# A decoder with mixture-of-experts routing: GpSimd's row transfers issued in gated fours

## The reference, cut to what matters

```python
x = x + L0_ffn(layernorm(x))        # 16 experts, top 4 of a token, and one shared expert
# inside: top_vals, top_idx = top_k(softmax(h @ router_w.T), 4)
#   comb[n, e] = weight of expert e for token n
#   y[e] = silu(h @ w_gate[e]) * (h @ w_up[e]) @ w_down[e]
#   routed = sum over e of y[e] * comb[:, e];  out = routed + sigmoid(h @ sh_gate_w) * shared
x = x + L1_attn(layernorm(x))       # 16 heads of 16 channels
x = x + L1_xattn(layernorm(x), ctx) # keys and values from ctx
x = x + L1_ffn(layernorm(x))
```

## Time and profile before

| | us |
|---|---|
| timed runs, median of 3 | 1796.05 |
| timed runs, lowest to highest | 1793.11 to 1799.43 |
| profiled execution, its own time | 1811.18 |
| profiled execution, span of its instructions | 1809.4 |
| PE busy in it | 1610.7 (89%) |
| DVE busy | 1128.6 (62%) |
| ACT busy | 972.1 (54%) |
| GpSimd busy | 540.4 (30%), with 128 row transfers |

### The profile page before, as it was taken

The page is one execution under the profiler, slowest core; times in us unless marked ns, Lnnn a source line. Parts: engine busy times, 40 slices in busy tenths (PEclk is TensorE's granted clock), DMA queues, the critical chain, the costliest instruction groups (busy, mean ns, idle before and its releaser), DMA issues. The chain is left out here.

```text
span 1809.4 us, 25838 instructions
## 1 busy us (share of the span) xinstructions
PE 1610.7 (89%) x8598; PEld 1292.1 (71%) x8598; DVE 1128.6 (62%) x2496; ACT 972.1 (54%) x2789; POOL 540.4 (30%) x447
## 2 busy tenths in 40 slices
PE   6999989989988868799998869999789999999866
PEld 4888877878877656677776637777668888788634
DVE  4655685776687585354443564544357788777878
ACT  4645545545445544223323546678746666667756
POOL 2233332553363462221103356354021122211000
PEclk9999999999999989999999958898789999999989
DMA  8153344433543052153434311000031110000001
GB/s 274 36 176 128 112 142 137 141 129 105 192 154 120 30 163 76 47 149 113 124 105 129 99 47 38 21 1 24 1 137 30 32 41 33 13 1 1 1 1 47
DMA packets 87511, 151.50 MB, mean 84 GB/s; under 512 B 9940, under 2 KB 45396, under 8 KB 87380
## 3 DMA queue, kind: packets, MB, share of 16 engines
q1 hardware_dynamic: 81236, 133.07, 22.6%
q0 software_dynamic: 6144, 16.79, 2.9%
HBM read 90.84 MB, written 58.98 MB: 83 GB/s over the span
## 5 line engine op out<-in xcount | busy, mean ns | idle before, releaser
L2598 ACT ACTIVATE cross_attention_heads<-cross_attention_heads,small 128x128 f32<-128x128 f32 x256 | 99.6, 390 | 89.3 <-DVE small L2033 89.3
L2342 ACT ACTIVATE self_attention<-self_attention,small 128x128 f32<-128x128 f32 x256 | 99.9, 392 | 79.7 <-DVE small L1666 79.7
L1126 PE MATMUL bank<-cross_attention,cross_attention_heads 128*128 128x256 f32 x512 | 125.0, 387 | 15.3 <-DVE residual L2047 10.1
L790 PE MATMUL bank<-self_attention 128*128 128x256 f32 x512 | 122.2, 381 | 17.4 <-ACT self_attention L2355 9.1
L2702 POOL CAST qkv_weights_split<-self_attention 128x1024 fp32r<-128x1024 f32 x45 | 49.2, 1093 | 253.4 <-DMA self_attention<-in_wqkv 231.4
L595 PE MATMUL bank<-x_channel_major,qkv_weights_split 128*128 128x512 f32 x256 | 117.1, 458 | 7.6 <-DVE qkv_weights_split L1698 2.9
L1126 PEld LDWEIGHTS bank<-cross_attention,cross_attention_heads 128*128 128x128 f32 x512 | 95.9, 192 | 38.8 <-DVE residual L2047 19.0
L2510 ACT ACTIVATE narrow_late<-bank,small 128x128 f32<-128x128 f32 x256 | 91.1, 376 | 58.8 <-DVE small L1904 58.3
L790 PEld LDWEIGHTS bank<-self_attention 128*128 128x128 f32 x512 | 95.5, 190 | 35.7 <-DVE residual L1680 13.8
L2704 POOL TENSOR_TENSOR qkv_weights_split<-self_attention,qkv_weights_split 128x1024 fp32r<-128x1024 f32 x45 | 109.1, 2423 | 3.7
L888 PE MATMUL bank<-experts,tiles 128*128 x316 | 108.0, 465 | 0.4 <-DVE tiles L1782 0.4
(11 more groups left out here) (398 smaller groups left out, 4716.2 us busy)
## 6 DMA issues: line engine op xcount, KB each, us to landing
picked_inputs<-self_attention SPq DMA_DIRECT2D x64, 512.0 KB, 6.7
self_attention<-in_wqkv SPq DMA_DIRECT2D x48, 512.0 KB, 6.1
experts_far<-picked_inputs SPq DMA_DIRECT2D x79, 128.0 KB, 2.1
picked_outputs<-tiles SPq DMA_DIRECT2D x79, 128.0 KB, 1.7
self_attention<-in_wo SPq DMA_DIRECT2D x16, 512.0 KB
experts<-in_moe SPq DMA_DIRECT2D x4, 1408.0 KB
self_attention<-in_bv SPq DMA_DIRECT2D x16, 256.0 KB, 5.7
context_values<-context_out SPq DMA_DIRECT2D x16, 256.0 KB
```

The costliest lines, as they stand in the source:

```text
L790: m = T.matmul(bank[7][:, 0:D], ZT_a[n % 2][:, h, :], wo_a[p % 2][:, h, :], start=h == 0, stop=h == HG - 1)
L1126: m = T.matmul(bank[7][:, 0:D], ZT_x[n % 2][:, h, :], x_wo[hg % 2][:, h, :], start=h == 0, stop=h == HG - 1)
L2342: m = S.activation(P_a[u][:, h, :], P_a[u][:, h, :], ACT.Exp, bias=negmax_a[u][:, h:h + 1], accum_out=sums_a[u][:, h:h + 1])
L2598: m = S.activation(P_x[u][:, h, :], P_x[u][:, h, :], ACT.Exp, bias=negmax_x[u][:, h:h + 1], accum_out=sums_x[u][:, h:h + 1])
```

## The change

Two waits are added to GpSimd's program. `scatter(g, b)` first waits until all transfers of the batches before b, from the start of the dispatch, have landed. In the loop over `gather(0)` to `gather(6)`, each but the first is preceded by a wait until the batch before has landed whole. `slow_scatter`, gather 7 and 8 and the later single picks stay as they are.

```diff
             def scatter(g, b):
+                pool.wait_ge(scattered, 16 * TOPK * (g * GB + b))
                 for k in range(TOPK):
                     scatter_pick(g, b, k)
...
             for bb in range(7):
+                if bb:
+                    pool.wait_ge(gathered[(bb - 1) % NYG], 16 * TOPK * ((bb - 1) // NYG + 1))
                 gather(bb)
```

## The result

| | before | after |
|---|---|---|
| median of 20 timed runs each | 1793.49 us | 1800.62 us |
| lowest to highest | 1790.04 to 1801.75 | 1789.28 to 1807.09 |
| ratio after/before, 95% interval | | 1.003 (1.0016 to 1.0044) |
| profiled execution, own time (span) | 1811.18 (1809.4) | 1795.7 (1793.9) |

The timed runs became 0.3% longer (5.4 us by the ratio), while the profiled execution became 15.5 us shorter. Both are true.

The account below looks back on a forecast made before the run. TensorE, busy 89% of a 1809.4 us span, was taken to bound the kernel. The forecast was 1796.05 - 0 for the gaps + 0 to 1 for the waits, rounded to 1796.0 us, range 1784 to 1802.

Parts of the forecast that it names:

- the price of the waits: Fourteen waits before scatters and gathers on GpSimd: 1.86 us each with work in flight, 0 to about 2 us altogether.
- group 2, +0.57 taken as 0: Expert-loop scatters: only the last batch follows closely, +0.57 us; taken as 0, or 0.6 if nothing hides it.
- the gathers, 0 to 1: Waits ahead of gathers 1 to 6, before the second self-attention: mostly covered, cost 0 to 1 us.
- one landing of 2.83 us: Issue to landing of a row transfer, read at gather 8's fourth transfer and used for every gated batch.
- the account of the gaps: Late waits after long rows of scatters and gathers: most timed executions lack them, they come with the profile's recording.
- the agreement it stood on: Profiled execution less its two gaps, 1811.18 - 15.4 = 1795.8 us, was close to the timed median of 1796.05.
- The size of the gaps, 15.4 us: Excess waits after sixteen scatters (4.1 us, TensorE) and twenty gathers (11.35 us, VectorE), together 15.4 us.
- Rival 1: The gaps are in timed runs too and fours cure them: 1781 to 1790 us; chance 0.28.
- Group 3, 0,: Three effective waits in group 3's scatters, 1.86 us each, covered by TensorE's remaining expert units: cost 0.
- rival 2: Landing is slower than thought, gathers reach past square(0): +5.1 us at 4.0 us landing, 1801 to 1804; chance 0.14.
- Rivals 3 and 4: 3: gap lasts as long as GpSimd issues, 1805 us or more, chance 0.05. 4: waits do nothing, 1796, chance 0.03.

Follow-up runs that it names:

- after_third: The changed kernel, unchanged, run again on a chip where the kernel before shows no gaps: 1799.35 us against 1793.98, ratio 1.0017.
- before_fourth: The kernel before, unchanged, run again on a chip where it shows no gaps: 1793.16 us against 1793.98, ratio 0.9989.

## Why the prediction was wrong

The time of 1800.62 us lies in the stated range, but no change was forecast, with 0 to 1 us for the waits, and the change cost 5.4 us (2.9 to 7.9 by the interval).

**The step that failed is the price of the waits**, in two terms: group 2, +0.57 taken as 0, is 2.2 (point 4), and the gathers, 0 to 1, are 2.6 (point 6). Both stood on one landing of 2.83 us, where it is 5.3 and 3.3. A second step, the account of the gaps, failed beside it (point 1), but what was drawn from it, that the timed runs have none, holds for this first measurement; that was luck in the chip.

1. **"Most timed executions don't have them, they come with the recording"** failed as an account, together with the agreement it stood on: 1811.18 less 15.4 is 1795.8, near the median of 1796.05. On chips A and B the timed runs are as long as the profiled ones, 1808.56 us and more. The profile of before has the gaps (own time 1811.18, below the middle of chips A and B but within their span), and the timed runs are like those of C and D. That they came from two kinds of chip is an inference, for those chips aren't known, and a change with time would fit as well. The agreement itself was luck in its size, since the gaps are worth 21.2 us, and a chip without them gave a profiled span of 1788.4.

2. **The size of the gaps, 15.4 us**, was a term too small by 5.8. For the first I took 6.97 less the 2.90 of the turn before it; the same turn costs 1.25 without a gap, and another 2.2 us is lost behind it, at the lower clock. For the second I counted to the eleventh key bias (11.35 where the whole row loses 13.1).

3. **Rival 1**, that fours cure gaps which timed runs have, is what happens on chip A: 0.9923, less than all of the gaps for the price of the waits. The case against it was point 1. In the first measurement it isn't what decided, as there was nothing to cure.

4. **Group 2, +0.57 taken as 0**, was mis-sized: 2.2. I used the landing of a gather in a quieter stretch, 2.83, where these scatters land in 5.3. The prediction itself put the price at 0.6 if nothing hides it, and took 0 without a row that showed something hiding it; of the 3.2 us for which GpSimd stands, 2.2 reach TensorE. The stretches of after_third say what stands beside them, the last two numbers being DMA share and GB/s:

```profile
640.00:660.00 20.00, 15.11 (x66) 11.10 (x65) 15.13 (x15) 8.66 (x13) 15.40 (x14) 1.00 1.13 295
...
720.00:760.00 40.00, 38.75 (x173) 30.85 (x172) 19.11 (x54) 12.13 (x21) 16.70 (x17) 1.00 0.20 66
```

The DMA engines are full in the first (share 1.13, 295 GB/s) and lightly used in the second (0.20), where group 3 lands in 2.36. The split behind group 2's last four on GpSimd then starts late, as the prediction named.

5. **Group 3, 0,** was right. Its three waits are 1.70 each (1.86 said), and its cover holds: from the L852 near 710 us to the first L879 it is 55.2 us both in after and in before_fourth.

6. **The gathers, 0 to 1,** are 2.6, and the mechanism is rival 2's. I put its point of decision at a pitch of 7.27 us, a landing of 3.16; measured were 7.42 and 3.3, beside a DMA share of 0.44 to 0.55 in the stretches of after. As it said, square(0) comes right behind the last gather and combine(3) waits (3.01 us). By its own sum the squares come 1.0 us late at this pitch (972.58 + 6 x 7.42 + 4.76 = 1021.9, less 1018.5 and 2.4) and gather 3 lands 3.1 us past 998.8; the 2.6 lie between. So a rival with a chance of 0.14 decided this term, on 0.5 us of landing that I could have bracketed: the row used lies in a stretch with less DMA work (share 0.29 from 1052 to 1060). What spoke against it, that gather 9 stood behind the row used, was no match for the loads beside the first seven.

7. **Rivals 3 and 4** are out: the gap doesn't follow the length of the issue, as it vanishes on chip A when the gathers are stretched from 28 x 1.27 to 7 x 7.4 us; and ten of the waits hold GpSimd (one in group 2, three in group 3, six at the gathers).

The Trainium skill (DMA: Bandwidth & Descriptors, Anatomy of one DMA — SWDGE (gpsimd) path) gives an estimate of 2.3 us for such a transfer. The 2.36 of group 3 agree; the 3.3 and 5.3 of the busier stretches don't, and by this estimate both costs would have been nearly nothing.

The Trainium skill (Runtime: NRT & Kernel Launch, The ~15µs preamble/postamble breakdown) has 6.2 us between a profile's total and the reported time. Here the reported time is 1.8 or 1.9 us above the span in every execution, profiled or only timed (1795.7 and 1793.9, 1811.18 and 1809.4 in two profiled ones), so no part of the 15 us was due to that.

## What to carry to other kernels

Where a profile and the timed runs of the same program differ by the size of one feature, don't subtract the feature: take a second profile on another chip before building on either, and judge a change on both kinds if there are two. A wait for a landing is to be priced by the DMA share of its own stretch (here 2.4, 3.3 and 5.3 us for the same 128 KB), and by the first thing queued behind it on the waiting engine. Gate only the rows that need it: group 3 and the gathers without group 2 gave 0.9904 where there were gaps and 0.9998 where there were none. The whole change gave 0.9923 and 1.0017 there; the intervals overlap, but the 2.2 us of group 2's wait are seen in the distances.

## What the runs showed of the hardware

One program takes about 1815 us on two chips and 1794 to 1797 on two others, 1.1% apart, the same way in all executions on each. The difference is at two places, where GpSimd issues rows of 16 and 20 or more row transfers 1.27 us apart beside dense matmuls. There VectorE and ScalarE stand for updates which no instruction explains that ended shortly before, up to 12.2 us in the kernel before. TensorE then waits for them, and its granted clock falls to 0.50 and costs some 2 us more. A row of twelve gathers leaves 8.1 and 3.5 us of such waits, rows of eight and fours with 2 us between none, and group 3's scatters in fours none either. The same 128 KB of rows lands in 2.4 us beside a DMA share of 0.20, in 3.3 beside 0.44 to 0.55 and in 5.3 beside 1.1. Which part of the chip delays the updates, and whether the two kinds are kinds of chip or of time, stays open: no view shows it, and the runs only show what brings the waits about.
